# Expert stages with unrolled tiles and a reordered router, and earlier inputs for the stages between them

## The reference, cut to what matters

```
for sublayer in (mixer, moe0, latent attention, block of GQA + moe1):
    m = bidirectional WKV scans over the side input f      # "condition", independent of x
    h = (tanh(x / 2) + 1) * m                              # m carries the factor 1/2 of the sigmoid
    x = x + sublayer(h)
moe0:  shared expert + top 4 of 16 routed experts, sigmoid gate, weights normalised
       hidden = silu(h W1 * h W3) * route (routed), silu(h W1) * h W3 (shared); y = hidden W2
latent: low-rank q and kv, layer norm, 16 heads of 16, causal softmax, output projection
moe1:  top 2 of 8 experts, softmax gate, hidden = silu(h W1) * h W3 * route
```

## Time and profile before

| | us |
|---|---|
| median of 3 runs | 1300.31 (1295.31 to 1301.39) |
| the profiled execution | 1298.61 |
| its span | 1296.8 |
| TensorE busy | 1129.0 (87%) |
| VectorE, ScalarE, GpSimd busy | 809.0, 561.3, 342.2 |
| mean granted TensorE clock | 0.949 of full speed |

### The profile page before, as it was taken

How to read it: one execution, slowest core, us unless ns; L and a number is a source line. 1 busy time by engine, 2 the same in 40 slices (tenths; PEclk the granted TensorE clock), 3 DMA queues, 4 the chain that set the end, 5 groups by cost and what they waited for, 6 DMA issues and landing times. The chain is left out here.

```text
span 1296.8 us, 16339 instructions
## 1 busy us (share of the span) xinstructions
PE 1129.0 (87%) x4986; PEld 604.1 (47%) x4986; DVE 809.0 (62%) x1215; ACT 561.3 (43%) x1501; POOL 342.2 (26%) x348
## 2 busy tenths in 40 slices
PE   0289997899968999999978997987997879979998
PEld 0045553455534444444436773446853348644443
DVE  7799995999956676667664443696504974224222
ACT  4355664556542232323232454675724757410110
POOL 0336654266550000000010000575502755200000
PEclk9989999899987999999987999898998979979999
DMA  7000000000033000000130001200000000000000
GB/s 282 24 1 1 1 1 1 1 0 1 21 147 141 1 1 0 1 0 0 36 162 1 2 2 43 113 1 1 2 1 1 0 0 0 0 9 1 1 0 32
DMA packets 5491, 33.38 MB, mean 26 GB/s; under 512 B 528, under 2 KB 1936, under 8 KB 3536
## 3 DMA queue, kind: packets, MB, share of 16 engines
q1 hardware_dynamic: 5424, 32.61, 6.5%
HBM read 31.56 MB, written 1.05 MB: 25 GB/s over the span
## 5 line engine op out<-in xcount | busy, mean ns | idle before, releaser
L815 POOL TENSOR_TENSOR decays<-decays,scores 128x768 f32<-128x768 f32 x64 | 119.8, 1874 | 135.3 <-ACT decays L750 135.1
L1103 PE MATMUL ph<-h,weights 128*128 x256 | 116.9, 601 | 0.0
L583 PE MATMUL pg<-h,weights 128*128 (+1 forms) x136 | 67.0, 616 | 55.8 <-PEq L361 54.3
L2149 POOL TENSOR_TENSOR spare<-m,weights 128x256 f32<-128x256 f32 x80 | 91.1, 1158 | 91.5 <-DVE m L2170 90.5
L750 ACT ACTIVATE decays<-pcum,neg_cum 128x256 f32<-128x256 f32 (+1 forms) x256 | 86.2, 425 | 7.1 <-PE pcum L636 6.8
L883 DVE SCALAR_TENSOR_TENSOR conv<-px,pp,conv 128x510 f32<-128x510 f32 (+2 forms) x102 | 75.9, 744 | 16.0 <-ACT conv L722 13.6
L583 PE MATMUL px<-h,weights 128*128 x136 | 72.5, 658 | 13.0 <-DVE conv L883 13.0
L1160 ACT ACTIVATE up<-ph 128x512 f32<-128x512 f32 x44 | 26.3, 597 | 129.6 <-PE ph L1103 129.6
L1103 PEld LDWEIGHTS ph<-h,weights 128*128 128x128 f32 x256 | 49.4, 193 | 62.2 <-issue 62.2
L1407 POOL TENSOR_TENSOR prob_gqa<-prob_gqa,inverse_gqa 128x128 f32<-128x128 f32 (+1 forms) x128 | 62.0, 506 | 59.4 <-DVE inverse_gqa L1397 57.8
L1767 POOL MEMSET halves<- 64x64 f32 x4 | 0.6, 145 | 279.4 <-POOLq L1011 279.2
(11 more groups left out here) (350 smaller groups left out, 2588.1 us busy)
## 6 DMA issues: line engine op xcount, KB each, us to landing
weights<-in_w_mixer SPq DMA_DIRECT2D x2, 2048.0 KB, 18.6
weights<-in_w_moe SPq DMA_DIRECT2D x2, 1536.0 KB, 8.3
moe_rest<-in_w_moe SPq DMA_DIRECT2D x2, 1536.0 KB, 13.5
weights<-in_w_gqa SPq DMA_DIRECT2D x1, 3072.0 KB, 10.3
weights<-in_w_gqa SPq DMA_DIRECT2D x1, 2048.0 KB, 14.8
weights<-in_w_moe SPq DMA_DIRECT2D x1, 1920.0 KB, 8.7
weights<-in_w_mixer SPq DMA_DIRECT2D x1, 1536.0 KB, 12.4
weights<-in_w_moe SPq DMA_DIRECT2D x1, 1152.0 KB, 12.6
```

What stands on the lines that cost most here:

```text
L583: op = nc.tensor.matmul(out[0:m, :], w[:, col + k * m:col + (k + 1) * m], net.h[:, ds(i * PAIR + k * TOK, TOK)], start=(k == 0), stop=(k = ...
L815: nc.gpsimd.tensor_tensor(decays[:, head % 4], decays[:, head % 4], scores[:], ALU.mult).then_inc(decay_scaled, 1)
L1103: op = nc.tensor.matmul(out[:], wt[:, n * D + k * P:n * D + (k + 1) * P], net.h[:, ds(i * PAIR + k * TOK, TOK)], start=(k == 0), stop=(k = ...
L2149: op = nc.gpsimd.tensor_tensor(out[:, :, s, :], src[:, :, 1 - s, :], sin[:, None, s, :].to_broadcast([P, 4, HALF]), ALU.mult)
```

## The change

- The tiles of both pairs of an expert stage are one written-out sequence t = 0 to 2N - 1; the hardware loops of TensorE, ScalarE and VectorE are gone. `up_project(t)` stands before `down_project(t - 1)` across the pairs too.
- Router: TensorE runs `up_project` of two tiles (and in moe0 the shared tiles' `down_project` around the transposes) before the routing weights exist. VectorE's products of the two shared tiles stand inside the routing chain. The split is done in halves, the second behind tile S + 3. The condition steps begin with tile S, four a tile up to m = 4S - 1 in the first pair.
- x of pair 0 is completed in tile N. Behind tile N + 5 of moe0, tanh and product make `h` of pair 0 for the latent stage; in the latent stage, likewise, for the attention stage. These stages then make that of pair 1 alone.
- Latent stage: the ring has four banks; the order is project(0), score(0), project(1), and VectorE takes one key group of pair 1, the maximum of round 0, and then the rest.

The diff, cut; most of the removed lines are those of the kernel printed above:

```diff
+    if tag in net.inputs:
+        return net.inputs[tag]
-    def scalar():
+    def scalar(*pairs):
-        for pair in range(PAIRS):
+        for pair in pairs or range(PAIRS):
             s = slice(pair * PAIR, (pair + 1) * PAIR)
             nc.scalar.activation(net.h[:, s], net.x[:, s], ACT.Tanh, scale=0.5) \
                 .then_inc(half_tanh, 1)
...
+        TILES = PAIRS * N
+        NEXT = N + 5 if cfg.gate_product else None
+        tanh_next, make_next, _ = (condition_input(net, "_latent") if cfg.gate_product else
+                                   (None, None, None))
...
+            def up_project(t):
+                i, m = divmod(t, N)
                 pe.wait_ge(w_loaded(m), 16)
+                pe.wait_ge(hidden_ready, max(t - 1, 0))
                 wt = weight_tile(m)
+                for n, out in enumerate((ph1[t % 2], ph3[t % 2])):
                     for k in range(KT):
                         op = nc.tensor.matmul(out[:], wt[:, n * D + k * P:n * D + (k + 1) * P],
+                                              net.h[:, i * PAIR + k * TOK:][:, 0:TOK],
                                               start=(k == 0), stop=(k == KT - 1))
                 op.then_inc(h_up_ready, 1)
+            def spread_weight(t):
+                i, m = divmod(t, N)
+                if m < S:
+                    return
+                r = m - S
+                pe.wait_ge(sel_loaded, 16)
+                pe.wait_ge(parts_ready, i + 1)
+                pe.wait_ge(hidden_ready, max(t - 1, 0))
+                nc.tensor.matmul(pw[t % 2][:], sel[:, r * P:(r + 1) * P],
+                                 parts[:, i * TOK:(i + 1) * TOK], start=True, stop=True) \
+                    .then_inc(w_ready, 1)
+            def down_project(t):
+                i, m = divmod(t, N)
+                pe.wait_ge(hidden_ready, t + 1)
                 if m == 0:
                     pe.wait_ge(x_added, i)
+                    if i == 0:
+                        pe.wait_ge(score_ready if cfg.gate_product else exp_in, 1)
                 wt = weight_tile(m)
                 for k in range(KT):
                     op = nc.tensor.matmul(pout[k][:], wt[:, 2 * D + k * P:2 * D + (k + 1) * P],
+                                          hidden[:, t % 2, :], start=(m == 0), stop=(m == N - 1))
                 op.then_inc(down_done, 1)
+            def turn_route():
+                pe.wait_ge(route_cols_ready, 1)
+                for n in range(TOK_TILES):
+                    op = nc.tensor.transpose(proute[n // 4][0:E, n % 4 * P:(n % 4 + 1) * P],
+                                             pick[:, 0, n, :], net.ident[:])
+                op.then_inc(route_turned, 1)
+            up_project(0)
+            up_project(1)
+            if S:
+                down_project(0)
+            turn_route()
+            if S:
+                down_project(1)
+                up_project(S)
+                up_project(S + 1)
+            spread_weight(S)
+            spread_weight(S + 1)
+            down_project(S)
+            for t in range(S + 2, TILES + 1):
+                if t < TILES:
+                    up_project(t)
+                    spread_weight(t)
+                down_project(t - 1)
...
+            for t in range(TILES):
+                i, m = divmod(t, N)
+                if m >= S and cfg.gate_product:
+                    copy_up(t)
+                silu(t)
+                if t == NEXT:
+                    act.wait_ge(x_added, 1)
+                    act.wait_ge(down_done, N)
+                    tanh_next(0)
+                for n, unit in enumerate(units):
+                    if m == 1 + n * SECOND:
+                        unit.scalar_operands(i, turn(i, n))
+                    if m == 2 + n * SECOND:
+                        unit.scalar_exp(turn(i, n))
+            def times_up(t):
+                dve.wait_ge(up_copied, t // N * routed + t % N - S + 1)
+                v.tensor_tensor(mid[:, t % 2, :], up[:, t % 2, :], ph3[t % 2][:], ALU.mult) \
+                    .then_inc(mid_ready, 1)
+            def weigh(t, src):
+                dve.wait_ge(w_ready, t // N * routed + t % N - S + 1)
+                dve.wait_ge(down_done, max(t - 1, 0))
+                v.tensor_tensor(hidden[:, t % 2, :], src, pw[t % 2][:], ALU.mult) \
+                    .then_inc(hidden_ready, 1)
+            def hide_shared(t):
+                dve.wait_ge(act_ready, t + 1)
+                dve.wait_ge(down_done, max(t - 1, 0))
+                v.tensor_tensor(hidden[:, t % 2, :], act_out[:, t % 2, :], ph3[t % 2][:],
+                                ALU.mult).then_inc(hidden_ready, 1)
             if cfg.gate_product:
                 dve.wait_ge(score_ready, 1)
...
             last = per_token(top8[:, :, cfg.top - 1])
             link(v.tensor_tensor(one, score[:], last, ALU.is_gt))
             link(v.tensor_tensor(two, score[:], last, ALU.is_equal))
+            if S:
+                hide_shared(0)
             link(v.tensor_reduce(col[:, 0], one, AX_X, ALU.add))
             link(v.tensor_scalar(col[:, 0], col[:, 0], -1.0, float(cfg.top), ALU.mult, ALU.add))
             dve.wait_ge(zeroed, 3)
...
             link(v.tensor_tensor(two, two, three, ALU.mult))
+            if S:
+                hide_shared(1)
             link(v.tensor_tensor(one, one, two, ALU.add))
             link(v.tensor_tensor(one, one, score[:], ALU.mult))
             link(v.tensor_reduce(col[:, 0], one, AX_X, ALU.add))
...
+            def split_route(p):
+                cols = slice(p * TOK, (p + 1) * TOK)
+                rest, high = route[:, cols], parts[0:E, cols]
+                route_link(v.tensor_copy(high, rest))
+                route_link(v.tensor_tensor(rest, rest, high, ALU.subtract))
+                route_link(v.tensor_copy(part[:, cols], rest))
+                v.tensor_copy(parts[PR:PR + E, cols], part[:, cols])
+                route_link(v.tensor_tensor(rest, rest, part[:, cols], ALU.subtract))
+                v.tensor_copy(parts[2 * PR:2 * PR + E, cols], rest).then_inc(parts_ready, 1)
+            route_link = link
+            split_route(0)
+            def add_to_x(i):
+                dve.wait_ge(down_done, (i + 1) * N)
+                for k in range(KT):
+                    out = net.x[:, i * PAIR + k * TOK:][:, 0:TOK]
+                    op = v.tensor_tensor(out, out, pout[k][:], ALU.add)
+                op.then_inc(x_added, 1)
+            for i in range(PAIRS):
                 link = Links(dve, links, i, per)
                 steps = [step for n, unit in enumerate(units)
                          for step in unit.vector(link, i, turn(i, n))]
                 for m in range(N):
+                    t = i * N + m
                     if m >= S and cfg.gate_product:
+                        times_up(t)
+                        dve.wait_ge(act_ready, t + 1)
+                        weigh(t, act_out[:, t % 2, :])
+                    elif m < S and t >= S:
+                        hide_shared(t)
+                    elif m >= S:
+                        dve.wait_ge(act_ready, t + 1)
+                        link(v.tensor_tensor(mid[:, t % 2, :], act_out[:, t % 2, :],
+                                             ph3[t % 2][:], ALU.mult))
+                        weigh(t, mid[:, t % 2, :])
+                    if m == 0 and i > 0:
+                        add_to_x(i - 1)
+                    if t == S + 3:
+                        split_route(1)
+                    if t >= S:
+                        take(steps, 3 + (i == 0 and m < 4 * S))
+                    if t == NEXT:
+                        make_next(0)
                 assert not steps
                 link.check()
+            add_to_x(PAIRS - 1)
...
         p_down, p_var = ([scores[:, 2 * pair + n] for pair in range(PAIRS)] for n in range(2))
-        ring = [scores_t[:, 0], scores_t[:, 1], po[:], aux[:], scores[:, 0], scores[:, 1]]
+        ring = [scores_t[:, 0], scores_t[:, 1], po[:], aux[:]]
...
         tanh_h, make_h, h_ready = condition_input(net, "_latent")
+        tanh_next, make_next, _ = condition_input(net, "_gqa", net.kept)
...
             pe.wait_ge(slots_made, 2)
-            for pair in range(PAIRS):
+            def project(pair):
...
+            project(0)
+            for n in range(2):
+                pe.wait_ge(taken[n], USES // 2)
+            pe.wait_ge(c_ready, PAIRS)
+            score(0)
+            project(1)
             for n in range(2):
                 pe.wait_ge(taken[n], PAIRS * USES // 2)
             pe.wait_ge(pool_once, 8)
-            score(0)
             turn_max(0)
             for r in range(ROUNDS):
                 if r + 1 < ROUNDS:
...
         def _(act):
-            tanh_h()
+            tanh_h(1)
...
             nc.scalar.preload_act_table_set("exp_and_others")
+            act.wait_ge(x_added, KT)
+            tanh_next(0)
...
                 [P, KT * 2, LATENT]), ALU.subtract).then_inc(down_made, 1)
```

(53 more changed lines are left out.)

77 lines of the change are left out of this document (12 added, 65 removed).

## The result

The changed kernel takes **1288.45 us** (median of 7 runs, 1287.02 to 1289.16); the kernel before, run beside it on the same chip, 1300.31 (7 runs, 1293.99 to 1303.25). The ratio is 0.9921, 95% interval 0.9897 to 0.9946: faster by about 0.8%, where 1296.3 was forecast (stated range 1285 to 1303). The profiled execution is 1287.02 us, its span 1285.2, against 1298.61 and 1296.8 before. Note the two spreads, 2.1 us and 9.3 us: they are the first sign of where the time went.

The account below looks back on a forecast made before the run. TensorE, busy 87% of 1296.8 us, was taken as the bound, with only the seams between stages open. Terms summed to -3.2 us: 1295.4 from the profiled run, 1297.1 from the median, middle 1296.3; range 1285 to 1303.

Parts of the forecast that it names:

- rival A: First latent rounds: TensorE's clock stays up, 10.2 us less, giving 1286.1 us; chance 0.20.
- First expert stage, router: First expert stage: moving up(0) and up(1) ahead gains 3.9 us, VectorE's crowded tiles eat 3.9; 0.0.
- seam: Between the first expert stage's pairs: up(24) before down(23) removes TensorE's wait and drain; -1.1 us.
- The walk: Queue-by-queue estimate of the first expert stage: hidden(4) 0.9 us late, hidden(5) 0.1, hidden(6) 2.9.
- Bound +1.5: Upper bound of the first expert stage's router term, if three more matmuls run at half rate.
- rival B: Both expert stages' router gains arrive: VectorE keeps up, clock holds in the second; another 3.8+2.1 us, 1290.4; chance 0.12.
- Latent start: Start of the latent stage: h of pair 0 made early lets the first matmul start sooner; -1.4 us.
- attention start: Start of the attention stage: one product instead of two stands before h_norm; -1.2 us.
- Rival D: Latent and attention starts: early h does nothing, something else starts them; 2.6 us back, 1298.9; chance 0.10.
- Latent reorder: Latent stage: four banks, TensorE waits 1.8 us before g=3, turn_max(0) later; +0.9 us, bounds -3 and +2.
- Second expert stage: down(0) 2.0 us earlier, five half-rate matmuls give back 2.1, so +0.1; its pair seam -0.5.
- Rival C: project(1) and rounds 0 to 3: pauses drop the clock sooner, three more slow rounds, +13.2 us, 1309.5; chance 0.06.

Follow-up runs that it names:

- e2: The kernel before with only the new latent order (four banks, score(0) between the projections, maximum(0) behind one key copy): 1291.84 us, ratio 0.9942.
- e3: The changed kernel without the early h: h of both pairs made at the start of the latent and attention stages again; 1294.70 us, ratio 0.9975.
- e4: The changed kernel with the second half of the routing-weight split at tile 12 instead of tile 5: 1283.60 us, ratio 0.9886.
- e7: The changed kernel with ten unread filler matmuls behind the transposes of the second expert stage's router: 1289.79 us.
- e8: The changed kernel with the split's second half at tile 16, six extra conditioner steps at tiles 8 to 13, silu's table loaded early: 1284.36 us, ratio 0.9875.
- e11: The changed kernel again, unchanged: 1288.93 us, ratio 0.9916.
- e1: The changed kernel with the old latent order (six banks, score(0) after both projections, maximum(0) last on VectorE): 1292.94 us, ratio 0.9962.
- e5: The changed kernel with maximum(0) last in VectorE's queue, TensorE's order kept: median 1298.85 us, two runs near 1289, ten from 1297.5 to 1302.9; ratio 0.9994.
- e10: The kernel before again, unchanged, for a second profile: 1300.01 us in its one run.
- e6: e1 with four unread full-width matmuls between score(0) and turn_max(0), where TensorE waits: 1289.45 us.
- e12: The kernel before with two unread filler matmuls between score(0) and turn_max(0) of the latent stage: 1291.57 us, ratio 0.9957.
- e9: e8 with maximum(0) behind two key copies instead of one and five filler matmuls behind the second expert stage's transposes: 1284.54 us, ratio 0.9882.

## Why the prediction was off, point by point

The measured 1288.45 lies in the stated range, 7.8 us below the forecast. What came is rival A, which had a chance of 0.20.

**The step that failed** is that the latent rounds were taken out of the sum as unchanged, and their recovery left to rival A at 0.20, with the words "round 0 keeps its own pauses, and nothing in it is changed". The rounds gave 10.5 us where A had 10.2. That A's 1286.1 lies so near the profiled 1287.02 is partly luck: taken against the profiled run alone A comes to 1285.2, and the 2.6 us that the first expert stage missed its forecast by are partly offset by small gains elsewhere. Round 0's own pauses do not bring the clock down in the seven profiles with the new order (the changed kernel's, e2, e3, e4, e7, e8, e11: 20.97 or 20.98 each). All four with a wait of 2.0 to 2.7 us ahead of turn_max(0) have the fall (before, e1, e5, e10); e5 put that wait back and lost the gain, e6 and e12 filled it and got it back. Two profiles show that this wait is not all of it: in e9 the clock falls without it, and in e12 it falls shortly behind round 0's own 1.00 us wait. The prediction had seen both the half clock and the pause, and had noted for A that "the new order cuts that up". The second argument was there too, named in A's last sentence but hardly weighed: a kernel whose runs lie 6 us apart has something in it that falls now one way, now the other, and an edit on the spot of it will move the odds.

**First expert stage, router (0.0) and seam (-1.1): sizes off.** Together +1.5 in the profiled pair. The walk was right to 0.1 us in both waits. It missed what the wait does to the clock: down(6) and the up behind it ran at half rate in six of the seven profiles with this code. From down(6) to down(7) is 5.48 us at full clock (e5) and 6.90 to 7.05 in five of them, so 1.5 us; in e6 it is 8.49. The stage takes 275.0 to 276.4 in the six, 272.67 in e5. It had the table load at the place of before; in the unrolled code it comes only behind the wait for up(0); that looks like 1.3 us and cost too little to be seen. From the logits to the transposes are 19.37 us; with the table loaded early (e8) 19.16, but with the load left in its place the other profiles have 18.3 to 19.7. And the kernel before was at its long end in the profile, which is luck of the pair that was forecast. The router gain came out at the 3.9 us that were forecast (down(2) 30.05 after the logits, 33.95 before), but the other profiles with the old stage (e2, e10, e12) have down(2) at 32.5 to 33.0, so that against them it is 2.5 to 2.9. Their stages take 272.2 to 272.7; against these the change made the stage some 2.5 us or more longer. Bound +1.5 was too low; rival B fell, but e4 and e8 get its time by moving the split.

**Latent start -1.4, attention start -1.2:** right in kind and near in size, -1.8 and -1.8 by the table, +1.4 and +1.6 when taken back in e3. Rival D is out.

**Latent reorder +0.9:** a little low. The table's +1.0 is no clean number, for the kernel before itself takes 24.39 to turn_max(0) in one profile and 25.37 in the other (e10), at lower clock. Pairs with like clock give 1.34 (changed against e1) and 1.2 (e2 against e10). The wait ahead of g=3 was 1.26, not 1.8.

**Second expert stage +0.1 and -0.5:** right within 0.3 (-0.1 together against -0.4), and for the reason given: down(0) came 2.5 us earlier after the logits and the half clock took that back. e9 shows the other side, 2.7 us for five matmuls of filler.

**Rival C** (the pauses in the projections bring the clock down sooner) did not occur in the changed kernel. e9 shows that it is not far: there the clock does fall at turn_max(0). What stays open is why: e8 and e9 are alike up to the latent stage, and in it e9 only has one key copy ahead of the maximum and 1.0 us less waiting ahead of g=3; e8's profile holds the clock, e9's does not. How many of e9's other runs fall cannot be told, for their times overlap those of e8. What the chip sees in the one and not in the other was not found.

The Trainium skill (TensorE: Matmul & The Clock Gate, What's actually happening) says that full clock is what activity earns and that the watching does not restart with a kernel, so that the moment of a switch varies from run to run. The twelve runs of e5, 1289 and 1298 to 1303 with one and the same code, are compatible with that; no run here shows where the watching stood.

## What to carry to other kernels

When a stretch runs at half clock in the profile, look for the wait of TensorE just ahead of it, and price an edit that shortens or fills this wait by the whole slow stretch, not by the wait: here 2.0 to 2.7 us of waiting came with 3.1 to 11.5 us lost in the profiled rounds (e5, e1, the kernel before, e10). If the runs of a kernel are spread wider than its work can explain, make such a stretch your first suspect, and give the outcome "it holds now" a chance to match. And when work is moved into a waiting engine's time, walk the queue that feeds it: the same 3 us of VectorE work cost 4.2 us at tile 5, 0.9 at tile 16 and nothing at tile 12.

## What the runs showed of the hardware

- A fall of the clock can far outlast the wait ahead of it, though TensorE is busy: in the kernel before it was busy for all of 702 to 704 at a granted 0.50, and behind a 2.01 us wait the latent rounds stayed slow for 20 us (27 in e10, but 10 in e1 behind the same wait). In the expert stage a 2.9 us wait cost 1.5 us in five profiles, 3.0 in e6 and nothing in e5.
- Matmuls that nobody reads can pay: 4.46 us of them in a 4.49 us wait gave 2.7 us back (e9); 1.98 us of them in a 2.01 us wait brought the median down by 8.8 (e12).
- The eight transposes take 1.04 us at full clock and 1.88 at half.
- The fastest versions seen are e4, e8 and e9 (1283.6, 1284.4, 1284.5; they cannot be told apart). e4 is the change with one number altered.
